# Two layers on one core: the rotated keys get a second projection, and the second attention is divided without transposes

## The reference

```python
# layer 0, attention: two rotated query-key products are multiplied, no softmax
q1, k1, q2, k2, v = (x @ W.T for W in (Wq1, Wk1, Wq2, Wk2, Wv))     # 16 heads of 8
y1 = x1 * cos + x2 * sin;  y2 = -x1 * sin + x2 * cos                # rotation of q1, k1, q2, k2
pattern = where(causal, (q1 @ k1.T) / 8 * (q2 @ k2.T) / 8, 0)
y = (pattern @ v) @ Wout.T
# layer 0, experts: sigmoid gate, 2 of 8, gelu, and a shared expert
# layer 1, attention: softmax over every 4th key and the 8 neighbours on either side
scores = where(allowed, q * sigmoid(unity_scale) @ k.T / sqrt(8), -inf)
y = softmax(scores) @ v @ o_w + o_b
# layer 1, experts: softmax gate, 2 of 8 with capacity 2048, relu
```

## Time and profile before

| | |
|---|---|
| median of 3 runs | 1613.81 us (1611.47 to 1619.32) |
| the profiled execution | 1619.32 us, its span 1618.1 us |
| busy | PE 94%, PEld 68%, DVE 62%, ACT 61%, POOL 51% |
| mean granted TensorE clock | 0.98 |

### The profile page before, as it was taken

How to read it: one execution, slowest core, us unless ns; L and a number is a source line. 1 busy time by engine, 2 the same in 40 slices (tenths; PEclk the granted TensorE clock), 3 DMA queues, 4 the chain that set the end, 5 groups by cost and what they waited for, 6 DMA issues and landing times.

```text
span 1618.1 us, 46666 instructions
## 1 busy us (share of the span) xinstructions
PE 1514.8 (94%) x17931; PEld 1096.1 (68%) x17931; DVE 1000.2 (62%) x2191; ACT 986.5 (61%) x2039; POOL 830.3 (51%) x908
## 2 busy tenths in 40 slices
PE   7889989999999999999999889999998999999995
PEld 5544444444444999999778666666666999997663
DVE  7789989888876222222599957765664222224887
ACT  5757657777766545454454557677776454546773
POOL 7334468888875555555112210277764555553433
PEclk9999989999999999999999979999999999999998
DMA  9910000210002899998344310011112544542434
GB/s 316 416 59 2 5 24 30 103 32 31 30 28 36 214 247 245 264 249 233 97 121 116 84 49 3 12 49 46 46 46 49 99 88 93 98 80 81 131 108 125
DMA packets 296954, 169.31 MB, mean 105 GB/s; under 512 B 198080, under 2 KB 273216, under 8 KB 293792
## 3 DMA queue, kind: packets, MB, share of 16 engines
q1 hardware_dynamic: 246608, 128.19, 29.8%
q0 software_dynamic: 16832, 34.64, 6.3%
q10 hardware_dynamic: 33296, 3.50, 1.8%
HBM read 96.61 MB, written 69.63 MB: 103 GB/s over the span
## 4 chain that ended last, share of the span: by engine, by line
PE 62%; POOL 12%; issue 9%; DVE 9%; ACT 5%; DMA 2%; SPq 1%; POOLq 0%; DVEq 0%; ACTq 0%
PE ps L1889 14%; PE ps L1880 14%; POOL xd L631 6%; POOL s_S L664 5%; PE ps L1693 5%; PE ps L1784 4%; PE ps L1821 4%; PE ps L1921 4%; DVE s_RS L1356 3%; ACT s_PX L890 3%; PE ps L1909 3%; PE ps L1717 2%; PE ps L1831 2%; PE ps L1788 2%; PE ps L1850 2%
## 5 line engine op out<-in xcount | busy, mean ns | idle before, releaser
L824 ACT ACTIVATE s_S<-ps 128x512 f32<-128x512 f32 x384 | 208.5, 595 | 144.1 <-PE ps L1693 144.1
L631 POOL DMA_INDIRECT xd<-s_XN,s_slots x256 | 250.3, 978 | 84.6 <-issue 62.5
L1544 DVE TENSOR_TENSOR s_PP<-ps,s_S 128x1024 f32<-128x1024 f32 x192 | 234.1, 1219 | 55.8 <-PE ps L1693 37.7
L1693 PE MATMUL ps<-s_QM,s_KK 32*128 32x512 f32 x1536 | 246.6, 648 | 5.2 <-ACT s_S L824 2.6
L890 ACT ACTIVATE s_PX<-ps,s_scl 128x1024 f32<-128x1024 f32 x128 | 135.7, 1111 | 112.0 <-PE ps L1831 112.0
L905 ACT ACTIVATE s_HH<-ps,s_LG 128x256 f32<-128x256 f32 x284 | 125.2, 474 | 121.9 <-PE ps L1880 121.9
L648 POOL DMA_INDIRECT yd<-s_Y,s_to x142 | 136.1, 959 | 122.2 <-DVE s_Y L1486 97.8
L664 POOL TENSOR_SCALAR_AFFINE_SELECT s_S<-s_S 128x1024 f32<-128x1024 f32 x128 | 141.7, 1107 | 109.3 <-ACT s_S L824 108.9
L1356 DVE TENSOR_REDUCE s_RS<-ps 128x8 f32<-128x1024 f32 x128 | 150.3, 1216 | 65.9 <-PE ps L1788 65.8
L905 ACT ACTIVATE s_XN<-ps,s_b1s 128x256 f32<-128x256 f32 x256 | 113.5, 475 | 115.0 <-PE ps L1880 111.1
L648 POOL DMA_INDIRECT yd<-s_XN,s_to x128 | 122.6, 958 | 117.6 <-DVE s_XN L1486 95.7
(11 more groups left out here) (227 smaller groups left out, 2710.6 us busy)
## 6 DMA issues: line engine op xcount, KB each, us to landing
s_W<-in_ew SPq DMA_DIRECT2D x71, 576.0 KB, 4.6
s_X<-xd SPq DMA_DIRECT2D x540, 32.0 KB
xd<-s_zero SPq DMA_DIRECT2D x16, 1056.0 KB, 18.1
s_YG<-yd SPq DMA_DIRECT2D x32, 256.0 KB, 3.7
s_XN<-yd SPq DMA_DIRECT2D x32, 256.0 KB, 4.0
yd<-s_zero SPq DMA_DIRECT2D x7, 1056.0 KB, 27.8
s_XN<-in_x SPq DMA_DIRECT2D x8, 512.0 KB, 7.2
xd<-s_XN,s_slots POOLq DMA_INDIRECT x256
```

The costliest lines, as they stand in the source:

```text
L631: e.indirect_dma_start(out=xd, out_offset=bass.IndirectOffsetOnAxis(ap=m.slots[:, k, i:i + 1], axis=0), in_=m.XNp[:, i, 0:C + 1], in_offse ...
L824: e.mul(m.S1[u % 3][:, t * 512:(t + 1) * 512], m.PA[:, t * 512:(t + 1) * 512], 1.0 / 64.0).then_inc(s.ev1, 1)
L1544: e.tensor_tensor(m.PP[u % 4][:], m.PB[u % 2], m.S1[u % 3][:], ALU.mult).then_inc(s.prod, 1)
L1693: return e.matmul(out, m.KK[k][32 * r:32 * r + 32, kind, kc * P:(kc + 1) * P], m.QM[k][32 * r:32 * r + 32, kind, :, qc * P:(qc + 1) * P], ...
```

## The change

In layer 0 a key projection becomes what a query projection was: two matmuls, one with swapped columns, and DVE adds the halves; the shuffle and its wait go. The weights in SBUF grow from 6 to 8 matrices of 128 columns.

In layer 1 the two transposes go. ACT first multiplies the whole bank by a mask of the odd blocks of 16 partitions (`second_halves`, a new function, placed ahead of the exponentials of the next sequence). DVE then makes two arrays of 256 columns: DEN (denominators) and NUM (numerators), each the one half of the bank in the even blocks plus ACT's masked other half. DEN is shuffled so that the blocks of 16 change places, its reciprocal is taken over all 256 columns, and NUM is multiplied by it.

```diff
 def rotate(e, m, s, b, x):
-    if x % 2 == 0:
-        e.tensor_tensor(rt[:], m.PS[7], m.cs[:], ALU.mult).then_inc(s.rt, 1)
-    else:
-        e.tensor_tensor(rt[:].rearrange("p (k n) -> p k n", k=2), bcast(m.PS[7][:, 0:256], 1, 2),
-                        m.cs[:].rearrange("p (k n) -> p k n", k=2), ALU.mult).then_inc(s.rt, 1)
+    e.tensor_tensor(rt[:], m.PS[7], m.cs[:], ALU.mult).then_inc(s.rt, 1)
+    if x % 2 == 1:
...
-        e.stream_shuffle(m.KX[:], rt[:, 256:512], [p ^ 4 for p in range(32)]).then_inc(s.kx, 1)
-        e.wait_ge(s.kx, 2 * b + x // 2 + 1)
-        e.tensor_tensor(m.KK[b % 2][:, x // 2, :], rt[:, 0:256], m.KX[:], ALU.subtract).then_inc(s.ka, 1)
+        e.tensor_tensor(m.KK[b % 2][:, x // 2, :], rt[:, 0:256], rt[:, 256:512], ALU.add).then_inc(s.ka, 1)

 def projection(e, m, s, b, x):
-    if x % 2 == 0:
-        e.matmul(m.PS[7][:, 0:256], m.W0[:, 3 * x // 2, :], xt, start=True, stop=True)
-        e.matmul(m.PS[7][:, 256:512], m.W0[:, 3 * x // 2 + 1, :], xt, start=True, stop=True).then_inc(s.proj, 1)
-    else:
-        e.matmul(m.PS[7][:, 0:256], m.W0[:, 3 * x // 2 + 1, :], xt, start=True, stop=True).then_inc(s.proj, 1)
+    e.matmul(m.PS[7][:, 0:256], m.W0[:, 2 * x, :], xt, start=True, stop=True)
+    e.matmul(m.PS[7][:, 256:512], m.W0[:, 2 * x + 1, :], xt, start=True, stop=True).then_inc(s.proj, 1)

+def second_halves(e, m, s, b):
+    e.wait_ge(s.wv, 2 * b + 2)
+    if b >= 1:
+        e.wait_ge(s.yn, b)
+    e.mul(m.SEC[:], m.PS[6][:, 0:512], m.second_half).then_inc(s.sec, 1)

 def divide_second(e, m, s, o, b):
-    e.wait_ge(s.wv, 2 * b + 2)
-    o.mark(e.transpose(m.TM[:], m.PS[6]))
-    o.wait()
-    o.mark(e.reciprocal(m.RC[:].rearrange("p (b h x) -> p b h x", b=8, h=2), view(m.TM[:], 16, [[32, 8], [240, 2], [8, 2]])))
-    o.wait()
-    for hp in range(2):
...
-        o.mark(e.tensor_tensor(view(m.YM[:], 16 * hp, [[32, 8], [8, 2], [1, 8]]), value, one_over, ALU.mult))
+    first, second = m.PS[6][:, 0:256], m.PS[6][:, 256:512]
+    e.wait_ge(s.sec, b + 1)
+    den = o.mark(e.scalar_tensor_tensor(m.DEN[:], second, m.first_half, m.SEC[:, 0:256], ALU.mult, ALU.add))
+    o.mark(e.scalar_tensor_tensor(m.NUM[:], first, m.first_half, m.SEC[:, 256:512], ALU.mult, ALU.add))
+    o.wait(den)
+    o.mark(e.stream_shuffle(m.RC[:], m.DEN[:], [i ^ 16 for i in range(32)]))
+    o.wait()
+    o.mark(e.reciprocal(m.RC[:], m.RC[:]))
     o.wait()
     if b >= 1:
         e.wait_ge(s.o1, b)
-    e.transpose(m.YC[:], m.YM[:]).then_inc(s.yn, 1)
+    e.tensor_tensor(m.YC[:], m.NUM[:], m.RC[:], ALU.mult).then_inc(s.yn, 1)

 def sync_program(e, m, s):
-            e.dma_start(m.W0, a["w0"][:, 0:6 * P].rearrange("c (m n) -> c m n", m=6)).then_inc(s.w0, 16)
+            e.dma_start(m.W0, a["w0"][:, 0:8 * P].rearrange("c (m n) -> c m n", m=8)).then_inc(s.w0, 16)

 def scalar_program(e, m, s):
...
+        if 1 <= t < NB and t - 1 != MOE_AFTER:
+            second_halves(e, m, s, t - 1)
         if t < NB:
             exponents(e, m, s, t, 0)
...
+        if t == NB:
+            second_halves(e, m, s, NB - 1)
         if t == MOE_AFTER:
+            second_halves(e, m, s, t)
```

More of the change, by code:

```diff
@@ L219, in memory @@
     m.eoff = small[:, 146:154]
+    m.first_half, m.second_half = small[:, 158:159], small[:, 159:160]
     m.row = small[:, 160:302]
@@ L254, in memory @@
     w0 = sbx(at, "W0", [P, 9 * P + E])
-    m.W0 = w0[:, 0:6 * P].rearrange("p (m n) -> p m n", m=6)
+    m.W0 = w0[:, 0:8 * P].rearrange("p (m n) -> p m n", m=8)
     m.VG = w0[:, 8 * P:9 * P + E]
@@ L263, in memory @@
     m.VM = [sbx(at, f"VM{k}", [P, 2, 16, 32]) for k in range(2)]
-    m.KX = sbx(at, "KX", [P, 256])
     at.close()
@@ L331, in memory @@
     m.Q4.append(sbx(bt, "Q41", [P, 4, 256]))
-    m.YM = sbx(bt, "YM", [P, 256])
+    m.RC = sbx(bt, "RC", [P, 256])
     m.YC = sbx(bt, "YC", [P, 256])
@@ L350, in memory @@
     m.b1s, m.b2s = sbx(bt, "b1s", [P, E, 4]), sbx(bt, "b2s", [P, E, C])
-    m.TM = sbx(bt, "TM", [P, 512])
-    m.RC = sbx(bt, "RC", [P, 32])
+    m.SEC = sbx(bt, "SEC", [P, 512])
+    m.DEN, m.NUM = sbx(bt, "DEN", [P, 256]), sbx(bt, "NUM", [P, 256])
     bt.close()
@@ L425, in semaphores @@
         "scl_a", "scl", "max", "maxv", "neg", "mturn", "mvt"))
-    s.sc, s.ex, s.wv, s.yn, s.o1, s.given, s.kx = (sem(n) for n in ("sc", "ex", "wv", "yn", "o1", "given", "kx"))
+    s.sc, s.ex, s.wv, s.sec, s.yn, s.o1, s.given = (sem(n) for n in ("sc", "ex", "wv", "sec", "yn", "o1", "given"))
     s.zg = [sem(f"l_zg{k}") for k in range(NF)]
@@ L564, in sync_program @@
     a = m.a
-    e.dma_start(m.VG[:, 0:P], a["w0"][:, 6 * P:7 * P]).then_inc(s.wv0, 16)
+    e.dma_start(m.VG[:, 0:P], a["w0"][:, 8 * P:9 * P]).then_inc(s.wv0, 16)
     for k in range(8):
@@ L1376, in divide_second @@
 def divide_second(e, m, s, o, b):
-    e.wait_ge(s.wv, 2 * b + 2)
-    o.mark(e.transpose(m.TM[:], m.PS[6]))
-    o.wait()
-    o.mark(e.reciprocal(m.RC[:].rearrange("p (b h x) -> p b h x", b=8, h=2), view(m.TM[:], 16, [[32, 8], [240, 2], [8, 2]])))
-    o.wait()
-    for hp in range(2):
-        value = view(m.TM[:], 272 * hp, [[32, 8], [8, 2], [1, 8]])
-        one_over = view(m.RC[:], 2 * hp, [[4, 8], [1, 2], [0, 8]])
-        o.mark(e.tensor_tensor(view(m.YM[:], 16 * hp, [[32, 8], [8, 2], [1, 8]]), value, one_over, ALU.mult))
+    first, second = m.PS[6][:, 0:256], m.PS[6][:, 256:512]
[4 more added lines that the diff above has]
+    o.mark(e.stream_shuffle(m.RC[:], m.DEN[:], [i ^ 16 for i in range(32)]))
+    o.wait()
+    o.mark(e.reciprocal(m.RC[:], m.RC[:]))
     o.wait()
@@ L2125, in _constants @@
         sm[:, 154 + j] = (np.arange(P) // 8) % 4 == j
+    sm[:, 158] = (np.arange(P) // 16) % 2 == 0
+    sm[:, 159] = (np.arange(P) // 16) % 2 == 1
     c["c_small"] = sm
@@ L2185 @@
         w = g["L0_attn_" + n].T
-        mats += [w, w[:, swap]] if "q" in n else [w]
+        mats += [w, w[:, swap]]
     mats += [g["L0_attn_Wv"].T]
```

## The result

The changed kernel takes 1624.98 us (median of 4 runs, 1622.85 to 1626.98), the kernel before in the same comparison 1613.26 (4 runs, 1611.47 to 1619.32). The ratio is 1.0064, with a 95% interval from 1.0043 to 1.0086: slower, by 7 to 14 us. The forecast was 1632 and 18.5 us more. The profiled execution took 1622.38 us, its span is 1621.2 and the mean granted clock 0.991 (before: 0.98).

A forecast was written before the change was run, and what follows sets the result against it. PE sets the pace in layer 0's attention; DVE time is dear in the gate's stretch and the last eight periods. 10 + 0.7 + 6.4 + 1.4 = 18.5 us on the median of 1613.81 gives 1632; 8 in 10: 1618 to 1652.

The forecast's parts named there:

- Slower: Whole kernel: slower by more than 0.5%, 8 us, given a chance of 81%.
- start and layer 0: Start and attention of layer 0: the added key matmuls cost 10 us together, between 4 and 34.
- `x = 3` is covered by ACT's copies: Layer 0, second pair's keys: 0.37 of the added matmul's 0.43 us hides in a wait; 31 x 0.06 = 1.9 us remain.
- An unwaited `x = 1` costs 0.43: Layer 0, first pair's keys: in 18 cases without a PE wait for DVE the added matmul costs 0.43 us, 7.7 together.
- the first rival: Layer 0: nothing is covered, every added matmul costs 0.52, 32 us instead of 10, time 1654; chance 16%.
- The wait shrinks by as much as PE gains in work, so these 12 cost nothing: Layer 0, first pair's keys: in 12 of 30 cases PE waits for DVE, which loses 0.5 us of work; cost nothing.
- The second rival: Gate's stretch of layer 0: DVE sets the pace, stretch 5.7 us shorter; in all +6, time 1620; chance 15%.
- Layer 1 early: Layer 1, 23 periods up to 1487 us: added 1.37 us just fits the margin of 1.36; 0.7 us, at most 4.6.
- The chain's length: Layer 1, DVE's division from DEN to YC: 3.48 us, 1.37 more than before, with 1.68 for the reciprocal.
- The third rival: Layer 1 division: the reciprocal takes 2.23 us instead of 1.68, 15 us added, time 1648; chance 5%.
- The late periods: Layer 1, last eight periods: two full ones lose 2.3 us, the other six half of 1.37 each; 6.4, between 2.3 and 11.
- ACT's copy: Layer 1 division: ACT's masked copy is done before DVE needs it, cost nothing; DVE waiting for it would prove the forecast wrong.
- The tail: Last division of layer 1, with nothing beside it: the added chain costs 1.4 us in full.

The follow-up runs named there:

- DVE's relief alone: Old keys with the single matmul, but DVE subtracts the halves without shuffle and its wait (keys wrongly rotated), against the kernel before: 1656.91 us, ratio 0.9913.
- the early division alone: New division only for sequences 0 to 21, old keys, against the kernel before: 1673.87 against 1673.21 us, ratio 1.0.
- the twin without cover: New two-matmul keys only for the first pair's keys (x = 1), against the kernel before: 1681.3 us, ratio 1.0042.
- the best form: New two-matmul keys only for the second pair's keys (x = 3), old division, against the kernel before: ratio 0.9892 on one chip, 0.9911 on another.

## Why the forecast was right in sign and too large

**Slower: right**, but only one of the two reasons held. The late division costs time, as forecast; layer 0, which was to bring more than half of the loss, got shorter. The two halves erred in opposite ways: start and layer 0 came to -2.6 to -4.4 us instead of +10, the late part to +11 to +12 instead of +7.8. That 1624.98 us lies within the stated 1618 to 1652 is owed in part to their offsetting each other.

**`x = 3` is covered by ACT's copies: right.** 0.06 forecast, 0.0 to 0.11 measured, and the block behind it takes 1.07 us. **An unwaited `x = 1` costs 0.43: right** (14.21 and 14.64; 13.71 and 14.14). A full sequence was to lose 0.49 and lost 0.53. This refutes the first rival, full price.

**The term that was missing is the clock: this is the step that failed.** The earlier trace rows showed 0.96 in the gate's stretch and 0.99 behind it, and nothing in the sum asked what that was or whether the change would touch it; it was put at nothing without a reason. The trace has 20.5 us at 1.2 GHz in layer 0 (23.9 in the second execution) and none after the change. They do the work of half that time, so the price was some 10 us (12), and the change gave it back. Without it the sequences from 2 to 31 would have gone from 431.5 to 438.7 us, 7 more, and the forecast's 10 would have been near. Five sequences gave 13.4 us back, more than the clock alone: the waits ahead of the pieces went too.

**"The wait shrinks by as much as PE gains in work, so these 12 cost nothing": right in the sum, not case by case.** Without the clock, sequences 2 to 16 took 223.2 us after the change and 223.9 to 224.1 before: relief and added work, some 7 and 4 us alone, came to a gain of 0.7 to 0.9 together. The waits themselves fell from 16.2 to 9.4 us, but unevenly: the longest went from 2.58 us to 1.00, while in sequence 15 it was 0.72 us before (the first of these rows) and 0.83 after (the second), and sequences 14 to 16 lasted 14.35 to 14.47 us before and 15.11 after.

```profile
269.31 0.67 PE L1658 MATMUL ps<-s_XT,s_W 128*128 128x256 f32 x2 [0.72 <-DVE s_RT L1282]
```

```profile
259.41 0.67 PE L1661 MATMUL ps<-s_XT,s_W 128*128 128x256 f32 x2 [0.83 <-DVE s_RT L1294]
```

In sequence 15 the relief of 0.5 us was spent on the way. Here DVE and POOL stand beside each other after the change, at two places of that stretch:

```profile
255.39 1.10 POOL L664 TENSOR_SCALAR_AFFINE_SELECT s_S<-s_S 128x1024 f32<-128x1024 f32 x1
255.58 0.96 DVE L1232 TENSOR_SCALAR s_SC<-s_SC 128x72 f32<-128x72 f32 x1
...
260.88 1.09 POOL L664 TENSOR_SCALAR_AFFINE_SELECT s_S<-s_S 128x1024 f32<-128x1024 f32 x1
261.34 0.91 DVE L1299 TENSOR_TENSOR s_KK<-s_RT 128x256 f32<-128x256 f32 x1
```

and before, where the small operation of the gate came later against the mask:

```profile
265.28 1.11 POOL L664 TENSOR_SCALAR_AFFINE_SELECT s_S<-s_S 128x1024 f32<-128x1024 f32 x1
266.22 0.23 DVE L1219 TENSOR_SCALAR s_SC<-s_SC 128x72 f32<-128x72 f32 x1
```

The same operation takes 0.23 us or 0.96, and the add 0.91 instead of 0.43; the first ends 0.05 us behind POOL's mask, the add 0.28. With the shuffle gone they come earlier under it. The subtraction of before met the mask too, but less: its mean was 554 ns, the add's is 672. The Trainium skill, "SBUF — State Buffer" (Who interferes with whom), says that VectorE and GpSimd take a shared port pair as an exclusive lock, and that a VectorE instruction with two SBUF inputs contends with a GpSimd instruction that reads SBUF, as the mask does; the trace agrees for the add. That this alone held the waits up is argued from these rows and not shown; a kernel without the mask was not run.

**The second rival** (DVE sets the pace, 1620) came nearest in size. Its mechanism is half right: DVE's relief alone shortens the gate's stretch, by some 7 us. But the added matmuls took nearly all of that away again, and the clock, which the rival didn't have either, made the difference.

**Layer 1 early: right.** The margin of 1.36 us against 1.37 of added chain: the 21 periods took 279.5 us for 280.1 and 278.5, and the early division alone gives 1.0 (on the third chip, where the longer periods leave the old division a margin of mostly 1.5 to 1.8 us, so it is the weaker evidence). The other kernels with the old division on the first chip took 276.4 and 277.9 us, so 1 or 2 us may have been lost. DVE's waits behind the output projection fell from 2.4 us each to 0.88.

**The chain's length: right.** 3.48 us; the reciprocal took 1.75 where the line gave 1.68, while the shuffle began a little earlier than assumed. The third rival, 2.23 us, is out. The Trainium skill, "VectorE: DVE Perf Modes" (First, the fixed hardware budget), gives the reciprocal a repeat count of 8. The rows say (1753 - 929) / 128 = 6.4 ns a column, which at the page's 0.96 GHz are about six cycles, so the count can't be taken for cycles a column.

**The late periods: the mechanism right, the term too small.** 6.4 us forecast (11 was its upper end), 10.1 to 10.7 measured. The working let the six looser periods take up half of the added 1.37 us, since DVE has idle time in them. That time lies where DVE waits for PE, not between division and bias: PE's next weighing waits for the bias, which DVE adds right after the division. So some 1.0 of the 1.37 reaches PE in each period: 6.8 to 7.3 us in the seven stretches to YC 29, and the new wait itself is 8.2 us in 8 pieces. The stretch to YC 30 lost 3.3 to 3.4 us; 0.7 of it is ACT's copy, which the prediction had put at nothing and named as a sign of being wrong. **The tail: right**, 1.4 us forecast, 1.3 to 1.4 measured.

## What to carry to other kernels

Where a stretch shows a granted clock under 1, find what PE waited for ahead of it and give that its own term. Here a matmul whose place was covered by another wait (`x = 3`) cost next to nothing in the full sequences and kept the clock up, and the shuffle that it replaced relieved DVE; together the kernel became 0.9% faster, while the twin without cover (`x = 1`) made it slower. Where DVE's added time is to be hidden in its idle time, ask which piece of idle lies between the added work and the next result that another engine wants; a share of the sum over a stretch is no answer. And a change of two parts is to be judged part by part: the best form takes one half of one of them.

## What the runs showed of the hardware

- In a kernel whose PE is busy for over 90% of a stretch, single waits of 1.25 to 2.6 us were enough to go ahead of a fall to 1.2 GHz. The longest, of 2.58 us, had a fall behind it in each of the seven executions in which it occurred; one of 1.39 us, later in layer 0, had one in the six profiles with the old keys and in that of the relief alone, and none in two others.
- In both profiled executions of the kernel before, four pieces of layer 0 come at the same places, and one more in the second.
- Work of no use on PE holds the clock: with 61 unneeded matmuls layer 0 had no time at half speed, where the old keys on the same chip had 13.7 us (0.97 and 1.00 between 215 and 265 us). The five executions with a second matmul for `x = 3` in all sequences had none, the six with the old keys 10.2 to 23.9 us. Which matmul each piece depended on stays open.
- A second float32 matmul of 128x128 by 256 columns cost 0.43 us of the sequence where nothing covered it, measured by one in each (14.21 to 14.64 us).
- A reciprocal of 128x256 float32 takes 1.75 us on DVE, four times a product of the same size.
- On one chip the 21 periods with scatters took 276.4 to 280.1 us, on the two others 323 to 328, in every kernel; durations do not carry from chip to chip.
